# Expert outputs of a mixture-of-experts layer: rows shared by neighbouring experts move to the later one, and an accumulating store waits for the last store but one

## What is computed

```python
probs = softmax(x @ router_w.T); topk_w, topk_ids = top_k(probs, 8)
pos = cumsum(onehot, axis=0)[arange(N), flat_e] - 1      # place of a token in its expert
valid = pos < C                                           # C = 128 places per expert
g, u = xb @ w_gate, xb @ w_up                             # per expert: 128 x 256 by 256 x 192
y = (silu(g) * u) @ w_down                                # 128 x 192 by 192 x 256
routed = segment_sum(y[safe] * (flat_w * valid), tok)     # each token sums its experts' rows
out = x + routed + shared
```

## Time and profile before

| | |
|---|---|
| median of 3 runs | 2898.26 us (2896.7 to 2900.53) |
| profiled execution, its own time | 2931.61 us |
| its span, first to last instruction | 2929.8 us |
| mean granted TensorE clock | 0.957 |
| busy: TensorE, VectorE, ScalarE, GpSimd | 91%, 76%, 36%, 28% of the span |
| the expert stage | from about 2651 us to the end |

### The profile page before, as it was taken

The page is one execution under the profiler, slowest core; times in us unless marked ns, Lnnn a source line. Parts: engine busy times, 40 slices in busy tenths (PEclk is TensorE's granted clock), DMA queues, the critical chain, the costliest instruction groups (busy, mean ns, idle before and its releaser), DMA issues. The chain is left out here.

```text
span 2929.8 us, 60955 instructions
## 1 busy us (share of the span) xinstructions
PE 2673.7 (91%) x23496; PEld 2250.8 (77%) x23496; DVE 2222.5 (76%) x6041; ACT 1060.3 (36%) x1557; POOL 818.0 (28%) x862
## 2 busy tenths in 40 slices
PE   2799999999999999999999999999999999657876
PEld 2678888888888888888888888888888887537775
DVE  4468888888888888888888888888888887433332
ACT  3234334444444444344444444443334443211111
POOL 1000122232222232223222222222322222343334
PEclk7699999999999999999999999999999999858988
DMA  6275444444444444443444333444433432208876
GB/s 190 70 192 156 107 125 125 123 120 108 98 100 103 103 103 103 99 99 96 98 103 103 97 94 93 103 103 103 99 91 94 101 85 46 51 22 223 216 194 132
DMA packets 321190, 327.31 MB, mean 112 GB/s; under 512 B 45517, under 2 KB 302239, under 8 KB 320900
## 3 DMA queue, kind: packets, MB, share of 16 engines
q1 hardware_dynamic: 285380, 297.94, 39.7%
q0 software_dynamic: 33792, 19.17, 3.8%
q10 hardware_dynamic: 1728, 6.29, 0.7%
HBM read 182.21 MB, written 212.37 MB: 135 GB/s over the span
## 5 line engine op out<-in xcount | busy, mean ns | idle before, releaser
L681 ACT ACTIVATE exps<-second 128x1024 f32<-128x1024 f32 x512 | 525.7, 1027 | 758.8 <-PE second L1179 734.2
L564 POOL DMA_INDIRECT expert_slots<-row_mem,sidx x512 | 506.9, 990 | 1001.7 <-PE first L1161 660.9
L1259 PE MATMUL mixp<-w_h,r_part_h 128*128 128x256 f32 x3072 | 667.1, 298 | 11.4 <-DVE hid L945 6.5
L853 DVE TENSOR_REDUCE nm<-first 128x4 f32<-128x1024 f32 x508 | 619.0, 1219 | 34.5 <-PE first L1161 31.0
L1259 PE MATMUL mixp<-w_h,r_part_l 128*128 128x256 f32 x3072 | 610.6, 280 | 0.0
L1259 PE MATMUL mixp<-w_l,r_part_h 128*128 128x256 f32 x3072 | 610.1, 280 | 0.0
L1259 PEld LDWEIGHTS mixp<-w_h,r_part_h 128*128 128x128 f32 x3072 | 468.0, 189 | 62.1 <-DVE hid L945 23.6
L1259 PEld LDWEIGHTS mixp<-w_l,r_part_h 128*128 128x128 f32 x3072 | 469.4, 188 | 0.0
L1259 PEld LDWEIGHTS mixp<-w_h,r_part_l 128*128 128x128 f32 x3072 | 469.3, 188 | 0.0
L945 DVE SCALAR_TENSOR_TENSOR x_mem<-mixp,C,x_mem 128x256 f32<-128x256 f32 x768 | 334.7, 477 | 75.5 <-PE mixp L1259 70.5
L945 DVE SCALAR_TENSOR_TENSOR hid<-mixp,C,hid 128x256 f32<-128x256 f32 x704 | 301.6, 477 | 108.3 <-PE mixp L1259 107.9
(11 more groups left out here) (225 smaller groups left out, 3628.1 us busy)
## 6 DMA issues: line engine op xcount, KB each, us to landing
kst<-k_parts SPq DMA_DIRECT2D x256, 192.0 KB
qst<-q_parts SPq DMA_DIRECT2D x256, 192.0 KB
q_parts<-nat_h SPq DMA_DIRECT2D x128, 256.0 KB
k_parts<-ctx_part_h SPq DMA_DIRECT2D x64, 256.0 KB
k_parts<-nat_h SPq DMA_DIRECT2D x64, 256.0 KB
q_parts<-nat_l SPq DMA_DIRECT2D x64, 256.0 KB
exps<-in_wgu SPq DMA_DIRECT2D x39, 384.0 KB
expert_slots<-row_mem SPq DMA_DIRECT2D x16, 642.0 KB, 6.5
```

Source lines behind the costliest of these rows:

```text
L564: pool.e.indirect_dma_start(out=slots_dram, out_offset=bass.IndirectOffsetOnAxis(ap=sidx[b % 2][:, t, k:k + 1], axis=0), in_=row[b % 2][:, ...
L681: act.e.activation(exps[:, j % NU, :, :, :].rearrange("p k t s -> p (k t s)"), second[:, :, :].rearrange("p k s -> p (k s)"), ACT.Exp, sca ...
L853: dve.e.tensor_reduce(nm[u % 2][:, :, 2 * j:2 * j + 2].rearrange("p t k -> p k t"), (mixp_mem if in_mixp(b, kind, j) else first)[:, :, :]. ...
L1259: m = pe.e.matmul(mixp[q % 2][:, t * D:(t + 1) * D], src[i][:, dt, t * P:(t + 1) * P], wmix[n][j][:, l, dt, :], start=(k == 0), stop=(k == ...
```

## The change

`e_same` now runs for every expert from 1 on and compares it with the one in front of it. Rows in common are added to the later expert, and the earlier one's number is set out of bounds, so that its store skips that row. Two neighbours therefore never name a common row, whichever two they are. A store waits for the last but one, by two semaphores, one for even and one for odd experts.

```diff
-        if e < NE and e % 2:
-            yield ("e_same", e // 2)
+        if 1 <= e < NE:
+            yield ("e_same", e)
...
-        c_w, c_init, c_add = sem("weights_in"), sem("slots_init"), sem("combine")
+        c_w, c_init, c_add = sem("weights_in"), sem("slots_init"), sems("combine", 2)
...
-                        sp.wait_ge(v_id, 2 * ((e - NX) // 2 + 1))
+                        sp.wait_ge(v_id, e - NX + 1)
...
-                elif what == "e_down" and a[0] % 2:
-                    pair = a[0] // 2
+                elif what == "e_down":
+                    e, = a
                     pool.wait_ge(c_out[0], 16 * (NB // 2))
                     pool.wait_ge(c_out[1], 16 * (NB // 2))
-                    pool.wait_ge(c_init, 16 * (NE // EMPTIED + 2))
-                    pool.wait_ge(v_id, 2 * (pair + 1))
-                    pool.wait_ge(c_add, 32 * pair)
-                    for e in (2 * pair, 2 * pair + 1):
-                        pool.wait_ge(v_ey, e + 1)
-                        pool.e.indirect_dma_start(
-                            out=out_pad, out_offset=bass.IndirectOffsetOnAxis(ap=eid[e % NID], axis=0), in_=ey[e % NY],
-                            in_offset=None, bounds_check=T + 2 * P - 1, oob_is_err=True, compute_op=ALU.add).then_inc(
-                                c_add, 16)
+                    pool.wait_ge(v_id, e + 1)
+                    pool.wait_ge(c_add[e % 2], 16 * (e // 2))
+                    pool.wait_ge(v_ey, e + 1)
+                    pool.e.indirect_dma_start(
+                        out=out_pad, out_offset=bass.IndirectOffsetOnAxis(ap=eid[e % NID], axis=0), in_=ey[e % NY],
+                        in_offset=None, bounds_check=T - 1, oob_is_err=False, compute_op=ALU.add).then_inc(c_add[e % 2], 16)
...
-                    dve.wait_ge(c_add, 32 * max(0, pair - NID // 2 + 1))
-                    dve.e.tensor_copy(eid[high % NID], high_no).then_inc(v_id, 1)
+                    if e > NID:
+                        dve.wait_ge(c_add[(e - 1) % 2], 16 * ((e - 1 - NID) // 2 + 1))
+                    dve.wait_ge(v_id, e - 1)
                     dve.e.tensor_tensor(id_step, spare_row, low_no, ALU.subtract).then_inc(*seq.up())
-                    dve.wait_ge(t_same, pair + 1)
-                    dve.wait_ge(t_dup, pair - 1)
+                    dve.wait_ge(t_same, e)
+                    dve.wait_ge(t_dup, e - 2)
                     dve.wait_ge(t_ht, NB)
-                    dve.e.tensor_scalar(same[pair % 2], attn_out[:, 0:P], low_no, None, ALU.is_equal).then_inc(v_same, 1)
+                    dve.e.tensor_scalar(same[e % 2], attn_out[:, 0:P], low_no, None, ALU.is_equal).then_inc(v_same, 1)
...
                     if e >= NY:
-                        dve.wait_ge(c_add, 32 * ((e - NY) // 2 + 1))
+                        dve.wait_ge(c_add[e % 2], 16 * ((e - NY) // 2 + 1))
...
-                    if e % 2:
+                    if e:
                         dve.e.tensor_scalar(ey[e % NY], y, w, None, ALU.mult).then_inc(*seq.up())
                         dve.wait_ge(v_seq, seq.n)
-                        dve.wait_ge(t_dup, e // 2 + 1)
+                        dve.wait_ge(t_dup, e)
...
                     pe.wait_ge(a_out, HALVES)
-                    pe.wait_ge(v_same, pair)
-                    pe.e.transpose(attn_out[:, 0:P], erow[high % NX][:, ROW - 1:ROW].broadcast_to([P, P]), ident).then_inc(
+                    pe.wait_ge(v_same, e - 1)
+                    pe.e.transpose(attn_out[:, 0:P], erow[e % NX][:, ROW - 1:ROW].broadcast_to([P, P]), ident).then_inc(
...
-                    if e % 2:
+                    if e:
                         pe.wait_ge(v_ey, e)
-                        pe.wait_ge(v_same, e // 2 + 1)
+                        pe.wait_ge(v_same, e)
                         pe.wait_ge(v_max, 4 * HALVES)
-                        pe.e.matmul(bank1[1][:, 0:D], same[e // 2 % 2], ey[(e - 1) % NY], start=True, stop=True).then_inc(
+                        pe.e.matmul(bank1[1][:, 0:D], same[e % 2], ey[(e - 1) % NY], start=True, stop=True).then_inc(
```

More of the change, by code:

```diff
@@ L475, in sync_program @@
                         sp.wait_ge(v_ey, e - NX + 1)
-                        sp.wait_ge(v_id, 2 * ((e - NX) // 2 + 1))
+                        sp.wait_ge(v_id, e - NX + 1)
                         sp.e.dma_start(erow[e % NX], slots_dram[e * CAP:(e + 1) * CAP, :]).then_inc(c_er[e % NX], 16)
-            sp.wait_ge(c_add, 16 * NE)
+            for s_ in c_add:
+                sp.wait_ge(s_, 8 * NE)
             sp.wait_ge(c_init, 16 * (NE // EMPTIED + 2))
@@ L567, in gpsimd_program @@
                         oob_is_err=False).then_inc(c_scat[b % 2], 16)
-                elif what == "e_down" and a[0] % 2:
-                    pair = a[0] // 2
+                elif what == "e_down":
+                    e, = a
                     pool.wait_ge(c_out[0], 16 * (NB // 2))
                     pool.wait_ge(c_out[1], 16 * (NB // 2))
-                    pool.wait_ge(c_init, 16 * (NE // EMPTIED + 2))
-                    pool.wait_ge(v_id, 2 * (pair + 1))
-                    pool.wait_ge(c_add, 32 * pair)
-                    for e in (2 * pair, 2 * pair + 1):
-                        pool.wait_ge(v_ey, e + 1)
-                        pool.e.indirect_dma_start(
-                            out=out_pad, out_offset=bass.IndirectOffsetOnAxis(ap=eid[e % NID], axis=0), in_=ey[e % NY],
-                            in_offset=None, bounds_check=T + 2 * P - 1, oob_is_err=True, compute_op=ALU.add).then_inc(
-                                c_add, 16)
-            pool.wait_ge(c_add, 16 * NE)
+                    pool.wait_ge(v_id, e + 1)
[4 more added lines that the diff above has]
+                        in_offset=None, bounds_check=T - 1, oob_is_err=False, compute_op=ALU.add).then_inc(c_add[e % 2], 16)
+            for s_ in c_add:
+                pool.wait_ge(s_, 8 * NE)
         def scalar_program(act):
@@ L1028, in vector_program @@
                 elif what == "e_same":
[L1029 to L1033, removed]
-                    dve.wait_ge(c_add, 32 * max(0, pair - NID // 2 + 1))
-                    dve.e.tensor_copy(eid[high % NID], high_no).then_inc(v_id, 1)
+                    e, = a
+                    low_no, high_no = (erow[n % NX][:, ROW - 1:ROW] for n in (e - 1, e))
+                    dve.wait_ge(c_er[(e - 1) % NX], 16 * ((e - 1) // NX + 1))
+                    if e > NID:
+                        dve.wait_ge(c_add[(e - 1) % 2], 16 * ((e - 1 - NID) // 2 + 1))
+                    dve.wait_ge(v_id, e - 1)
                     dve.e.tensor_tensor(id_step, spare_row, low_no, ALU.subtract).then_inc(*seq.up())
-                    dve.wait_ge(t_same, pair + 1)
-                    dve.wait_ge(t_dup, pair - 1)
+                    dve.wait_ge(t_same, e)
+                    dve.wait_ge(t_dup, e - 2)
                     dve.wait_ge(t_ht, NB)
-                    dve.e.tensor_scalar(same[pair % 2], attn_out[:, 0:P], low_no, None, ALU.is_equal).then_inc(v_same, 1)
-                    dve.wait_ge(v_same, pair + 1)
-                    dve.e.tensor_reduce(id_flag, same[pair % 2], AX_X, ALU.max).then_inc(*seq.up())
+                    dve.e.tensor_scalar(same[e % 2], attn_out[:, 0:P], low_no, None, ALU.is_equal).then_inc(v_same, 1)
+                    dve.wait_ge(v_same, e)
+                    dve.e.tensor_reduce(id_flag, same[e % 2], AX_X, ALU.max).then_inc(*seq.up())
                     dve.wait_ge(v_seq, seq.n)
-                    dve.e.scalar_tensor_tensor(eid[low % NID], id_step, id_flag, low_no, ALU.mult, ALU.add).then_inc(v_id, 1)
+                    dve.e.scalar_tensor_tensor(eid[(e - 1) % NID], id_step, id_flag, low_no, ALU.mult, ALU.add).then_inc(v_id, 1)
+                    if e == NE - 1:
+                        dve.wait_ge(c_er[e % NX], 16 * (e // NX + 1))
+                        dve.wait_ge(c_add[e % 2], 16 * ((e - NID) // 2 + 1))
+                        dve.e.tensor_copy(eid[e % NID], high_no).then_inc(v_id, 1)
                 elif what == "e_gate":
@@ L1345, in tensor_program @@
                 elif what == "e_same":
-                    pair, = a
-                    high = 2 * pair + 1
-                    pe.wait_ge(c_er[high % NX], 16 * (high // NX + 1))
+                    e, = a
+                    pe.wait_ge(c_er[e % NX], 16 * (e // NX + 1))
                     pe.wait_ge(a_out, HALVES)
-                    pe.wait_ge(v_same, pair)
-                    pe.e.transpose(attn_out[:, 0:P], erow[high % NX][:, ROW - 1:ROW].broadcast_to([P, P]), ident).then_inc(
+                    pe.wait_ge(v_same, e - 1)
+                    pe.e.transpose(attn_out[:, 0:P], erow[e % NX][:, ROW - 1:ROW].broadcast_to([P, P]), ident).then_inc(
                         t_same, 1)
```

## The result

| | before | after |
|---|---|---|
| median (range, runs) | 2901.6 us (2896.7 to 2904.48, 6) | 2884.39 us (2878.85 to 2887.63, 6) |
| ratio, 95% interval | | 0.9941 [0.9927, 0.9955] |
| profiled execution, its own time / its span | 2931.61 / 2929.8 us | 2884.72 / 2883.0 us |

The change makes the kernel faster by 17.2 us, 0.6%, three times the 0.2% that can be told from nothing.

What follows compares the result with a forecast made beforehand. Waits for paired stores to land were taken to bound the expert stage. Afterwards the 7.84 us loop exceeds the stores' 7.5: 2659.4 plus 239.1 plus 10.7 gives 2909.2, scaled to 2878 us; range 2867 to 2893.

Steps and rivals of the forecast that it cites:

- The loop: Expert stage: TensorE and VectorE wait for each other once per expert; 3.92 us per expert, 7.84 per pair, expected to bind.
- The rivals of a cheap and a dear handshake: TensorE-VectorE handshake: cheap, stores bind, 2867 us, chance 0.09; dearer, 4.17 to 4.35 us per expert, chance 0.08.
- The end: From the start of expert 63's gate to the span's end: 10.7 us in place of 24.2, saving 13.5 us.
- The gain as a difference: Whole span: 20.6 us (0.70%) less than the profiled 2929.8 us, 7 from the pace and 13.5 from the end.
- Profiling loads the DMA: Rival: the 33 us between profile and median sit mostly in the stores, moving the result towards 2885 us; no chance given.
- The step that failed: Accumulating stores into `out`: waiting only for the last but one gives 7.5 us per pair in place of 8.50.
- Two stores hold each other up: Rival at the stores: each takes 8.5 us in a steady stream, only the tail shortens, 2896 us; chance 0.10.
- The clock falls: Rival in the loop: gaps lower TensorE's clock; gain gone at share 0.18, 2929 us at 0.4; chance 0.09, mostly slower.

Runs made afterwards that it cites:

- gate_first: Changed kernel with the gate of the expert in front moved ahead of each expert's transpose and comparison; 2883.47 us, 0.9833 of the kernel before on the same chip.
- four_same: Changed kernel with four buffers for the comparison matrix `same` in place of two; 0.9819 of the kernel before, and 0.9833 when repeated (_b) on another chip.
- pair_wait: Changed kernel with the old wait put back, each store waiting for every store ahead of its pair; 0.9942 of the kernel before, 0.9949 when repeated.
- pair_wait_four: Changed kernel with four `same` buffers and the old wait for pairs of stores put back; 2896.04 us, 0.9973 of the kernel before.
- before_split: Kernel before with only the new wait, odd experts stored into a second tensor and the halves not summed; 2846.67 us, 0.9806 of the kernel before.
- before_again: Kernel before, unchanged, profiled a second time on another chip; 2934.93 us, against a median of 2934.19 us there.

## Why the prediction was right, and where a step of it was wrong

2878 us was predicted, 2884.39 measured, inside 2867 to 2893. By the ratio, 0.9941 x 2898.26 is 2881 us.

**The loop** (3.92 us per expert, "what I expect to bind") was right: 236.5 us for 61 turns is 3.88. The handshake is 0.50 us, as summed (0.11 + 0.34 + 0.05 there, 0.10 + 0.36 + 0.04 here), and TensorE's own part 3.38 us, from one transpose's start to the product's end, where I had 3.42. gate_first and four_same show the loop as the cause. The rivals of a cheap and a dear handshake are out with it.

**The end** (10.7 us from the last gate, 13.5 saved) measured 11.5 and 12.7. Mis-sized by 0.8 us: the last store starts 7.6 us behind the gate's start, not 6.9. The quicker pace gave 10.0 us where I had 7.

**The gain as a difference.** 20.6 us were predicted, against the profiled execution. From gate 2 to the end of the span it is 270.6 us in the first profile of before and 247.9 in that of after, so 22.7 there. The medians give 17.2. What parts them is the length of the stage before, taken from one execution: 280.9 us there, 278.1 and 274.6 in two others (the last with skipped rows, which cost nothing). With 274.6 in its place the same loop and end would have given some 14 us (20.6 less 6.3, an estimate).

**Profiling loads the DMA**: wrong. Some 23 of 29 us lie in the earlier program, as on the slow chip, and 6 in the stage. Scaling the whole sum by 2898.26 / 2929.8 did no harm, as it takes 0.2 us off the gain, but its reason was wrong.

**The step that failed** is the one on stores: a cycle of "7.5 ... in place of 8.50", because a store waits for the last but one. I took 8.50 as what pairs of stores cost, so without the new wait nothing should have been gained. pair_wait has 7.84 us and the whole gain. The 7.5 was too long as well: without the handshake the new wait let pairs through in 6.73 us (four_same_b). The time came out in spite of this step, because the loop, at 7.84, is the longer term with either value. Pairs bind at 8.3 to 8.55 us only where compute stands at the `ey` buffers. In the changed kernel the handshake keeps it from there, so the visible gain is the handshake's slower beat in place of a worse one, and the new wait brings nothing. Its value comes out when the handshake goes (some 40 us, four_same_b against pair_wait_four).

**Two stores hold each other up**: refuted by before_split, 6.56 us for a pair whose stores take 5.7 each. The Trainium skill, DMA: Bandwidth & Descriptors, Rules for kernel authors, has it that transfers to disjoint halves serialize; taken as a rule for these stores, it would have left 8.50 us, and the run disagrees. That most of a store's time isn't transfer (1.14 of 4.70 us, an estimate from rows 4 and 5) fits this; the transfers themselves may well take turns, which no run tests.

**The clock falls**: it stood at 1.00 for 210 us. The Trainium skill, TensorE: Matmul & The Clock Gate, A second HAM failure mode, tells of micro-idles that made it oscillate; a rest of 0.30 us in 3.89 didn't do that here.

**What I didn't ask** is what the change could have given. Its own handshake took most of it: before_split, 57 us; the change without handshake, 50; the change, 17.

## What to carry to other kernels

When an edit puts a step in every turn that stood in every second one, count its buffers anew: two of `same` were enough for pairs, and with one comparison per expert they tied two engines into a loop worth 0.5 us a turn; four gave 32 us back. Test a gain against its cause before crediting it: here the new wait that seemed to bring it could be undone at no loss that could be told, because another wait had taken its place. And a pace read where compute stands at a buffer belongs to that state; the same stores ran quicker once compute came for another reason.

## What the runs showed of the hardware

- An accumulating indirect store of 128 rows took 4.70 us, from its start to that of the store that waited for it, with a quiet DMA, and 5.7 us (median; 3.7 to 7.1) to land in before_split with the DMA share at 0.97. Two in flight overlapped: a pair went through in 6.56 us there, and in 6.73 us in four_same_b (5.4 us to land).
- A rest of TensorE of 0.30 us in every 3.89 left the granted clock at 1.00, the 2.4 GHz level. In before it was 0.67 from 2732 to 2740 us, around a rest of 4.52 us. The rest's length alone doesn't decide: behind one of 1.68 us (2768 to 2770, clock 0.71) it fell too, behind one of 3.17 us (2760 to 2762, 1.00) it didn't.
- Whole kernels differ by chip: before took 2934 us on one and 2902 to 2904 on others, with ScalarE idle put down to "remote" for 43.3 us (22.2 + 21.1) in before_again's profile from the slower one, and such rows in all four profiles from it. Outside it only the first profile of before has them. Ratios were the same on both (pair_wait 0.9942, 0.9949; four_same 0.9819, 0.9833), so compare on one chip.
